# Binarized weights prepared on ScalarE and VectorE instead of VectorE alone, in an eight-core transformer layer

## The reference, cut to what matters

```python
# L0_attn_x: (8, 2048, 2048); 16 heads of 128; weight: (2048, 2048)
x = x + _layernorm(_L0_attn_ref(_layernorm(x), W_Q, W_K, W_V, W_O, b_Q, b_K, b_V, b_O))
x = x + _layernorm(_L0_ffn_ref(_layernorm(x), weight, bias))

def binarize_weight(w):
    alpha = jnp.mean(jnp.abs(w), axis=1, keepdims=True)     # one number per output row
    bw = jnp.where(w >= 0, 1.0, -1.0) * alpha
    return bw
# _L0_ffn_ref: einsum('bsi,oi->bso', x, binarize_weight(weight)) + bias
```

## Time and profile before

| | us |
|---|---|
| median of 3 runs | 2424.3 |
| the three runs | 2421.8, 2424.3, 2653.07 |
| profiled execution, its own time | 2422.95 |
| its span, from the first to the last instruction of the slowest core | 2421.4 |
| spans of the 8 cores | 2414.2 to 2421.4 |
| mean granted TensorE clock of the cores | 0.901 to 0.905 |

### The profile page before, as it was taken

The page is one execution under the profiler, slowest core; times in us unless marked ns, Lnnn a source line. Parts: engine busy times, 40 slices in busy tenths (PEclk is TensorE's granted clock), DMA queues, the critical chain, the costliest instruction groups (busy, mean ns, idle before and its releaser), DMA issues.

```text
span 2421.4 us, 27245 instructions; the slowest of 8 cores (2414.2 to 2421.4 us)
## 1 busy us (share of the span) xinstructions
PE 1874.2 (77%) x8336; PEld 804.0 (33%) x8336; DVE 989.4 (41%) x1760; ACT 554.4 (23%) x737; POOL 239.9 (10%) x558
## 2 busy tenths in 40 slices
PE   1566887978879788797887978879642699999995
PEld 1332333323333233332333323333222344444442
DVE  3433332333323333233332333323367655555553
ACT  2224032140321403214032140321400111111111
POOL 1001011010111101101011111110100000000000
PEclk9778898988989889898898988989865799999997
DMA  7231121211212122121121324232153123333221
GB/s 163 91 74 20 20 27 14 31 16 20 27 14 31 15 21 27 14 31 16 20 27 14 42 39 55 27 48 40 40 161 113 35 87 88 87 88 87 76 76 50
DMA packets 178475, 119.34 MB, mean 49 GB/s; under 512 B 168100, under 2 KB 168100, under 8 KB 170148
## 3 DMA queue, kind: packets, MB, share of 16 engines
q0 software_dynamic: 107200, 75.51, 17.7%
q1 hardware_dynamic: 71140, 42.07, 6.9%
HBM read 125.97 MB, written 25.17 MB: 62 GB/s over the span
## 4 chain that ended last, share of the span: by engine, by line
PE 65%; DVE 9%; ACT 9%; issue 8%; POOL 4%; DVEq 3%; DMA 2%; ACTq 0%; POOLq 0%; SPq 0%
PE psA L362 9%; PE psB L362 9%; PE psE L659 7%; ACT ptil L586 6%; PE psC L362 5%; PE psC L856 5%; PE psA L747 5%; PE psB L747 5%; PE psC L622 3%; DVEq L58 3%; POOL ptil L612 2%; PE psE L856 2%; PE psD L856 2%; PE psD L362 2%; PE psE L362 2%
## 5 line engine op out<-in xcount | busy, mean ns | idle before, releaser
L641 DVE TENSOR_TENSOR ptil<-ptil,c 128x512 bf16<-128x512 bf16 x640 | 220.4, 418 | 480.2 <-ACT c L631 461.8
L362 PE MATMUL psA<-arena_a,wbuf 128*128 128x512 bf16 x1024 | 304.2, 384 | 5.2 <-ACT arena_a L276 3.1
L362 PE MATMUL psB<-arena_a,wbuf 128*128 128x512 bf16 x1024 | 303.5, 383 | 3.2 <-ACT arena_a L276 3.2
L659 PE MATMUL psE<-ptil,v 128*128 128x512 bf16 x640 | 187.8, 389 | 52.3 <-DVE ptil L641 52.3
L622 PE MATMUL psC<-ptil,onem_sb 128*128 128x512 bf16 x640 | 182.5, 399 | 52.2 <-POOL ptil L609 25.0
L586 ACT ACTIVATE ptil<-psA,mbias 128x1024 bf16<-128x1024 f32 x160 | 178.3, 1114 | 182.8 <-PE psE L659 77.8
L612 POOL TENSOR_TENSOR ptil<-ptil,tri_sb 128x128 bf16<-128x128 bf16 x256 | 109.3, 427 | 889.9 <-ACT ptil L586 889.8
L490 ACT ACTIVATE srow<-srow 1x1 f32<-1x1 f32 x32 | 6.5, 203 | 821.5 <-DVE srow L485 821.5
L586 ACT ACTIVATE ptil<-psB,mbias 128x1024 bf16<-128x1024 f32 x160 | 177.2, 1107 | 0.0
L572 PE MATMUL psA<-qt,kt 128*128 128x512 bf16 x320 | 109.4, 427 | 78.4 <-ACT ptil L586 51.4
L856 PE MATMUL psC<-arena_a,c 128*128 128x512 bf16 x512 | 154.0, 383 | 17.2 <-DVE c L840 17.2
(11 more groups left out here) (125 smaller groups left out, 2199.1 us busy)
## 6 DMA issues: line engine op xcount, KB each, us to landing
c<-fw POOLq DMA_DIRECT2D x16, 1024.0 KB, 5.9
ptil<-x SPq DMA_DIRECT2D x16, 1024.0 KB, 8.3
out<-wbuf POOLq DMA_DIRECT2D x16, 1024.0 KB, 10.9
wbuf<-wq POOLq DMA_DIRECT2D x16, 512.0 KB, 6.9
wbuf<-wk POOLq DMA_DIRECT2D x16, 512.0 KB, 6.5
c<-x SPq DMA_DIRECT2D x8, 1024.0 KB, 4.9
wbuf<-wv POOLq DMA_DIRECT2D x16, 512.0 KB, 6.5
zs<-c SPq DMA_DIRECT2D x64, 128.0 KB, 1.9
```

The costliest lines, as they stand in the source:

```text
L362: e.matmul(banks[bidx], wslot[sl][:, c * 128:(c + 1) * 128], ln1t3[:, c, s * SLW:(s + 1) * SLW], start=(c == 0), stop=(c == NCH - 1)),
L641: dv_norm[j] = p.op("vector", lambda e, j=j, g=g: e.tensor_tensor(pslot[j], pslot[j], rbc[g % 2], ALU.mult), wait=wait, inc="DV")
L659: pe_av = p.op("tensor", lambda e, j=j, chunks=chunks: e.matmul(psE[:, 0:GQ], v_sb[:, j * 128:(j + 1) * 128], pslot[j], start=(j == 0), st ...
```

## The change

In stage 3 the sign is taken by ScalarE (an activation Sign from the float32 tile straight into v), VectorE multiplies v in place by alpha, and ScalarE copies the transposed banks to arena_a. The 0-or-1 pass and the second 128x1 number are gone. The load of tile t + 2 waits for the magnitude sum and the sign of tile t. ScalarE's sign waits for the transposes of the tile before, because they read v. Other waits that named VectorE's last copy now name ScalarE's. In stage 4 the normalized tiles of i = 0 and 1 also wait for the end of stage 3 on TensorE and ScalarE.

```diff
         if t - 2 in dv_fw_free:
-            wait = [("DV", dv_fw_free[t - 2])]
+            wait = [("DV", dv_fw_free[t - 2]), ("SC", sc_sign_d[t - 2])]
...
-        p.op("vector", lambda e: e.tensor_scalar(
-            twoal[:], asum[:], 2.0 / DM, None, ALU.mult))
-        p.op("vector", lambda e: e.tensor_scalar(
-            negal[:], asum[:], -1.0 / DM, None, ALU.mult))
-        p.drain("vector")
-        p.op("vector", lambda e, fpar=fpar: e.tensor_scalar(
-            fwst[fpar], fwst[fpar], 0.0, None, ALU.is_ge))
-        p.drain("vector")
-        dv_bw = p.op("vector", lambda e, fpar=fpar: e.tensor_scalar(
-            v_sb[:], fwst[fpar], twoal[:, 0:1], negal[:, 0:1],
-            ALU.mult, ALU.add), inc="DV",
+        dv_al = p.op("vector", lambda e: e.tensor_scalar(
+            twoal[:], asum[:], 1.0 / DM, None, ALU.mult), inc="DV")
+        dv_fw_free[t] = dv_as
+        w2 = [(FWs[fpar], fw_t), ("PE", pe_bw_last)]
+        if t == 0:
+            w2.append(("PE", pe_av_all[H - 1]))
+        sc_sign_d[t] = p.op("scalar", lambda e, fpar=fpar: e.activation(
+            v_sb[:], fwst[fpar], AF.Sign, bias=0.0, scale=1.0),
+            wait=w2, inc="SC",
...
+        dv_bw = p.op("vector", lambda e: e.tensor_scalar(
+            v_sb[:], v_sb[:], twoal[:, 0:1], None, ALU.mult),
+            wait=[("SC", sc_sign_d[t]), ("DV", dv_al)], inc="DV",
...
-            dv_bw_evac_half[half] = p.op(
-                "vector", lambda e, t=t, b=b, c0=c0, c1=c1: e.tensor_copy(
+            sc_bw_evac_half[half] = p.op(
+                "scalar", lambda e, t=t, b=b, c0=c0, c1=c1: e.copy(
...
-                wait=[("PE", pe_bw_last)], inc="DV")
+                wait=[("PE", pe_bw_last)], inc="SC")
...
-        if i == 1:
-            w3.append(("PE", B_PE))
+        if i < 2:
+            w3 += [("PE", B_PE), ("SC", B_SC)]
```

More of the change, by code:

```diff
@@ L309, in build_program @@
     pe_w_done_d = {}
-    dv_bw_evac_half = [0, 0]
-    dv_bw_evac_last = 0
+    sc_bw_evac_half = [0, 0]
+    sc_sign_d = {}
     dv_fw_free = {}
@@ L342, in emit_w_mms @@
                                  ("SC", sc_rinv_prev),
-                                 ("DV", max(dv_bw_evac_half)),
+                                 ("SC", max(sc_bw_evac_half)),
                                  ("DV", dv_qkv_evac_d.get((h, 0), dv_bank_free))]
@@ L401, in emit_bw_tile @@
     def emit_bw_tile(t):
-        nonlocal dv_bw_evac_last, pe_bw_last
+        nonlocal pe_bw_last
         fpar = t % 2
@@ L410, in emit_bw_tile @@
             wait=wait, inc=FWs[fpar], incn=16)
-        w = [(FWs[fpar], fw_t)]
-        if t == 0:
-            w.append(("PE", pe_av_all[H - 1]))
         dv_as = p.op("vector", lambda e, fpar=fpar: e.reduce_sum(
             asum[:], fwst[fpar], AX.X, apply_absolute_value=True),
-            wait=w, inc="DV")
+            wait=[(FWs[fpar], fw_t)], inc="DV")
         p.drain("vector")
-        p.op("vector", lambda e: e.tensor_scalar(
-            twoal[:], asum[:], 2.0 / DM, None, ALU.mult))
-        p.op("vector", lambda e: e.tensor_scalar(
-            negal[:], asum[:], -1.0 / DM, None, ALU.mult))
-        p.drain("vector")
-        p.op("vector", lambda e, fpar=fpar: e.tensor_scalar(
-            fwst[fpar], fwst[fpar], 0.0, None, ALU.is_ge))
-        p.drain("vector")
-        dv_bw = p.op("vector", lambda e, fpar=fpar: e.tensor_scalar(
-            v_sb[:], fwst[fpar], twoal[:, 0:1], negal[:, 0:1],
-            ALU.mult, ALU.add), inc="DV",
+        dv_al = p.op("vector", lambda e: e.tensor_scalar(
[7 more added lines that the diff above has]
+            wait=w2, inc="SC",
             lowp="binarized weight is a bf16 matmul operand")
-        dv_fw_free[t] = dv_bw
+        dv_bw = p.op("vector", lambda e: e.tensor_scalar(
+            v_sb[:], v_sb[:], twoal[:, 0:1], None, ALU.mult),
+            wait=[("SC", sc_sign_d[t]), ("DV", dv_al)], inc="DV",
+            lowp="binarized weight is a bf16 matmul operand")
         hn2 = max(NCH // 2, 1)
@@ L435, in emit_bw_tile @@
             c1 = NCH if half else hn2
-            wait = [("DV", dv_bw), ("DV", dv_bw_evac_half[half]),
+            wait = [("DV", dv_bw), ("SC", sc_bw_evac_half[half]),
                     ("DV", dv_zevac.get(gidx - 1, 0))]
             for c in range(c0, c1):
-                w2 = wait if c == c0 else ()
+                w3 = wait if c == c0 else ()
                 tgt = p.op("tensor", lambda e, c=c, b=b, c0=c0: e.transpose(
@@ L442, in emit_bw_tile @@
                     v_sb[:, c * 128:(c + 1) * 128],
-                    eye_sb[:]), wait=w2, inc="PE" if c == c1 - 1 else None)
+                    eye_sb[:]), wait=w3, inc="PE" if c == c1 - 1 else None)
             pe_bw_last = tgt
-            dv_bw_evac_half[half] = p.op(
-                "vector", lambda e, t=t, b=b, c0=c0, c1=c1: e.tensor_copy(
+            sc_bw_evac_half[half] = p.op(
+                "scalar", lambda e, t=t, b=b, c0=c0, c1=c1: e.copy(
                     bwt3[:, c0:c1, t * 128:(t + 1) * 128],
@@ L449, in emit_bw_tile @@
                                                       c=c1 - c0)),
-                wait=[("PE", pe_bw_last)], inc="DV")
-        dv_bw_evac_last = dv_bw_evac_half[(2 if NCH > 1 else 1) - 1]
+                wait=[("PE", pe_bw_last)], inc="SC")
     def emit_mh_sq(which, h):
@@ L657, in build_program @@
                     wait += [("DV", dv_zevac.get(gidx - 1, 0)),
-                             ("DV", max(dv_bw_evac_half))]
+                             ("SC", max(sc_bw_evac_half))]
                 pe_av = p.op("tensor", lambda e, j=j, chunks=chunks: e.matmul(
```

## The result

The changed kernel takes 2399.1 us (median of 10 runs), the kernel before 2434.95 in ten runs beside it; these medians contain disturbed runs, in which some cores had a lower granted clock, and the ratio leaves them out: it is 0.9883, with a 95% interval of 0.9841 to 0.9925. By the 2% that was set, this is no change; by the interval the kernel is 0.75 to 1.6% faster. The forecast was 2396 us, 1.1% faster. The profiled execution took 2398.66 us with a span of 2396.8, against 2422.95 and 2421.4.

What follows compares the result with a forecast made beforehand. VectorE was taken to pace stage 3, 8.25 us per tile in a row; 6.0 per tile, with load waits and 3.5 given back, starts row tile 1's projection 27.3 earlier: 2422.95 - 27.3 = 2395.7, given as 2396, range 2389 to 2409.

Steps and rivals of the forecast that it cites:

- the load of tile 3: Stage 3 weight load: issued about 1767.8 us, landing at 1781, so tile 3's transposes start at 1784.7.
- the ring: Stage 3's per-tile chain through VectorE, ScalarE and TensorE: 6.0 us per tile in place of 8.25.
- the stretch: From the start of tile 0's sum to row tile 1's projection (L747), forecast to start at 1874.05, 27.3 us earlier.
- T0: Start of tile 0's transposes in stage 3 (T1 to T15 likewise): 1762.3 us against 1764.20.
- T4: Start of tile 4's transposes, where row tile 0's projection follows: 1790.7 us against 1799.00.
- T5 to T6: Tile 5's transposes to tile 6's, right behind row tile 0's projection: 5.6 us.
- Load 2: Tile 2's weight load: issued about 1761.5 us, landing near 1773, so T2 is 1776.8 in place of 1774.3.
- The wait at the end: Row tile 1's projection waits for psA and psB copies behind ScalarE's 16 tiles: 5.15 us after T15, giving back 3.5.
- Slow sign or multiplication: Rival, stage 3: multiplication 1.35 us, or sign 2.28 too; 2403 or 2407 us in all; chance 0.10.
- Loads: Rival: weight loads of 12.3 us set stage 3's pace, 7.4 us a tile, 2408 us in all; chance 0.09.
- Table swaps: Rival: ScalarE reloads tables between Sign and Copy, 8.6 us per tile, 2427 us in all; chance 0.04.
- better than forecast: Case: tile 2's load lands by 1771 us, T4 is 1786.3, 4.4 us less, 2391 in all; chance 0.07.

Runs made afterwards that it cites:

- e11: Changed kernel with row tile 0's x load issued behind tile 8's transposes, zs and x of row tile 1 following it: 2400.6 us.
- e12: Changed kernel with ScalarE's psA and psB copies of row tile 0 moved to behind sign 5, ahead of tile 5's copies: 2395.2 us.
- e1: Changed kernel with the two copies per tile back on VectorE, the sign staying on ScalarE: 2395.2 us.
- e2: Kernel before, nothing moved between engines, the sum of tile t + 1 put ahead of tile t's copies on VectorE: 2403.2 us.
- e4: Changed kernel with row tile 0's psA and psB copies directly behind the projection's call, so ahead of sign 5: 2399.1 us.
- e5: Changed kernel with copies back on VectorE and the sum of tile t + 1 ahead of tile t's copies: 2385.5 us.
- e7: Against the kernel before: sign on ScalarE, two v tiles, sum ahead, copies split over two engines, row tile 0's projection in pieces: 2369.5 us.
- e13: e7 with a third weight load buffer, x and zs loads behind tile 9, psA and psB copies behind tile 14's copy: 2350.7 us.
- e3: Kernel before with only the copies moved to ScalarE, binarization staying on VectorE in its old form: 2395.2 us.
- e6: Changed kernel with only the call of row tile 0's x load moved behind tile 8; the load was issued at the old time: 2399.1 us.
- e9: e3 with a third buffer for the weight's loads: 2387.5 us.

## Why the prediction was right, and where it was not

The mechanism and most terms held; two statements did not: that the load of tile 3 would hold the ring up, and that nothing behind the stretch would change. The forecast stretch on core 2 is 1874.05 - 1758.64 = 115.4 us; 115.0 was measured. Term by term, the measured ones from the changed kernel's rows above and its timeline:

| term | forecast | measured |
|---|---|---|
| T0 behind the first sum | 3.7 | 3.6 |
| transposes to first copy | 1.11 | 1.11 |
| copy, copy, sign, apart | 0.92, 0.92 | 0.91, 0.90 |
| sign | 1.86 | 1.92 |
| sign to multiplication | 0.10 | 0.18 |
| multiplication | 0.75 | 0.75 |
| multiplication to transposes | 0.36 | 0.39 |
| ring, tiles 6 to 15 | 6.02 | 6.16 |
| T4 | 32.1 | 30.5 |
| T4 to T5, the projection | 18.5 | 18.0 |
| T5 to T6 | 5.6 | 5.7 |
| T15 to the next projection | 5.15 | 5.3 |

**The ring.** Right in its links; nine rings at 0.14 more are 1.3 us late (the other seven cores have 6.12 to 6.13). The mis-sized term is the sign and its hand-over, 1.92 + 0.18 for 1.86 + 0.10. The multiplication, which no row of before had, was found at 0.75, the value taken, at the low end of its bounds.

**The loads.** Load 2 was right: its sum started 14.5 us behind the first (1775.60 - 1761.06), 14.4 forecast, and T2 came at 18.3 for 18.2. Load 3 was mis-sized and did not bind. It was to land 13.2 us after its issue and put T3 1.9 us behind the ring; it was in use 11.2 us after its issue (1769.68 on GpSimd, 1780.83), 19.8 behind the first sum and not 22.4, and T3 followed T2 by 6.12, the ring's own pace. So T4 came 1.6 us early. On cores 6 and 7 loads 3 and 4 did cost time beyond the ring (T4 at 28.2 to 33.0 over the eight cores). e11 bears out the cause that was named, the loads of stage 4.

T4 is 1.6 us early and the projection of row tile 0 0.5 shorter; the ring is 1.3 late, T5 to T6 and the end 0.2 together. That the sum comes within 0.4 us of 115.4 is partly luck.

**The wait at the end.** 3.5 us forecast; 5.3 in place of 1.66 is 3.6, and e12 removes it. But the prediction let nothing behind L747 change except its start, and there it was wrong: after that wait the projection of row tile 1 ran longer at the granted clock of 0.50, 17.5 us for 16.0 on core 2, 1.3 more by the medians of the cores. In the kernels without the wait (e1, e2, e4, e5, e7, e12, e13) the medians are 15.9 to 16.8, in those with it (changed, e3, e6, e9, e11) 16.6 to 17.4.

**The reading of the parts.** The forecast priced the change as one ring and said that the sum now runs while TensorE and ScalarE work. That is right: e2 has 20.5 of the 26.8 us from this alone. But it did not ask what each move is worth alone, and there its picture was incomplete. Either half gives no less than both: e1 113.9, e3 112.2, both 115.1. The halves do not add: each, done alone, already breaks the old chain, and both together put two copies and the sign on the same engine one behind the other, 1.01 + 1.02 + 1.92 us of ScalarE in a ring that VectorE alone had walked in 5.3 (e9).

**The rivals.** Slow sign or multiplication: refuted, 1.92 and 0.75. Loads: not in the changed kernel behind tile 4, with a ring of 6.12 and a load that lands 5.1 us after its issue (median; 5.9 before); but this rival is real, and e3, e7 and e11 meet it. The Trainium skill's rule of a load held while VectorE runs a two-port mode (SBUF — State Buffer, SBUF: two separate sides) is not shown by any run here: the issue does fall under the multiplication, and the loads landed sooner than before. Table swaps: refuted; the changed program, too, has one table load in all,

```profile
L221 ACT ACT_TABLE_LOAD  x1: 1283/1283/1283, 22.9 to 22.9; - x1
```

so Sign came with the table that Ln and Exp use. The case "better than forecast" (tile 2 by 1771) did not occur on core 2.

The time itself came out 3 us above 2396, although the stretch was 0.4 shorter than forecast. On core 2 the span went from 2421.4 to 2396.8, 24.6 us less: the stretch gave 27.7, stage 3 began 2.4 later than before (1761.06 for 1758.64), before any instruction that the change touches, the projection was 1.5 longer, and the rest 0.8 shorter. Over the cores the start lies between 1753.3 and 1760.0 before, 1755.1 and 1761.1 after; I take it for spread, and it was not studied.

## What to carry to other kernels

Where every engine of a stage is half idle, write the ring down with each link's own duration and ask first which instruction can be moved up in its engine's list: one sum moved ahead of two copies gave three quarters of what the whole change gave. Do each half of a two-part change alone: here the two remedies for one chain did not add. A call emitted early in an in-order list blocks what stands behind it, and on an idle engine a DMA issue goes by its waits and not by where the call stands: look in the trace whether the edit moved what it was to move. And the largest piece of this stage was none of the tile's operations but a block of 18 us in TensorE's list; cutting it into the gaps, together with a second v tile, shared copies and a third buffer for the loads, made the version that beats both.

## What the runs showed of the hardware

- ScalarE's Sign on 128x2048 float32 in SBUF takes 1.92 us, only 0.06 above what its copies out of PSUM give by their columns (1.86). Its end is seen by VectorE 0.18 us later, for 0.10 behind a 128x1 operation.
- In the changed kernel TensorE's granted clock is 0.50 (1.2 GHz) over a window of 60.70 us in which it is busy 18.65 us, with over 4 us of idle in each tile. In e13 on core 7 it is 0.51 up to 1779.70 and 1.00 (2.4 GHz) from there to 1798.70. Just before it rose, TensorE had worked without a gap from 1774.17, on the transposes of tile 4 and the first piece of the projection. It stayed at 1.00 while TensorE was busy 12.99 of the 19.00 us. Eight transposes then took 0.61 us in place of 1.01:

```profile
1782.27 0.61 PE L484 MATMUL psD<-eye_sb,v 128*128 128x128 bf16 x8 [0.95 <-DVE v L460]
...
1784.03 0.59 PE L809 MATMUL psA<-arena_b,qt 128*128 128x512 bf16 x2
```

- So the pieces of the projection cost less than at the half clock by which e7's expectation priced them, 0.59 us for two matmuls in the row above.
- The same clock has a price at the other end: behind 3.42 us of idle the changed kernel's projection of row tile 1 began at 0.50 and took 17.5 us, where the one before, right behind the transposes, took 16.0.
